# A graph attention kernel: the Sign taken from rows to columns, and the units of work cut the other way

## The reference

```
h  = max(layernorm(x), 0)
Wh = h @ W;  s = Wh @ a1;  t = Wh @ a2          # a1, a2: the halves of a
e  = leaky_relu(s[:, None] + t[None, :], 0.2)
att = softmax(where(adj > 0, e, -9e15), axis=1)
out = x + elu(att @ Wh)
```

## Time and profile before

| | |
|---|---|
| runs, median (lowest to highest) | 693.45 us (692.99 to 693.48) |
| the profiled execution, its own time | 694.66 us |
| its span, first to last instruction | 692.8 us |
| PE, DVE, ACT busy | 91%, 90%, 91% of the span |
| adj, 128 tiles of 2 MB, moved at | 427 GB/s in the loop |
| granted clock of PE, mean | 0.986 of full |

### The profile page before, as it was taken

How to read it: one execution, slowest core, us unless ns; L and a number is a source line. 1 busy time by engine, 2 the same in 40 slices (tenths; PEclk the granted TensorE clock), 3 DMA queues, 4 the chain that set the end, 5 groups by cost and what they waited for, 6 DMA issues and landing times.

```text
span 692.8 us, 23845 instructions
## 1 busy us (share of the span) xinstructions
PE 632.5 (91%) x10422; PEld 621.6 (90%) x10422; DVE 621.0 (90%) x625; ACT 631.4 (91%) x366; POOL 53.4 (8%) x51
## 2 busy tenths in 40 slices
PE   4867999999998989989898998989898998989895
PEld 4747999999998989989898998989898998989895
DVE  5898979999999899898989899898989989898983
ACT  4797999999999989989898998989899898989881
POOL 5000001011000101010010101001010100001010
PEclk9987999999999999999999999999999999999998
DMA  9876899999999999999999999999999999999960
GB/s 323 360 292 260 347 374 386 422 429 425 428 425 430 427 427 429 424 430 425 429 424 429 428 427 425 427 429 425 429 427 426 428 426 429 424 429 427 427 293 19
DMA packets 24840, 275.15 MB, mean 397 GB/s; under 512 B 3088, under 2 KB 7440, under 8 KB 8432
## 3 DMA queue, kind: packets, MB, share of 16 engines
q1 hardware_dynamic: 22864, 270.67, 93.3%
q0 software_dynamic: 1488, 4.07, 1.5%
q10 hardware_dynamic: 464, 0.07, 0.1%
HBM read 272.70 MB, written 2.10 MB: 397 GB/s over the span
## 4 chain that ended last, share of the span: by engine, by line
DMA 32%; DVE 29%; ACT 22%; issue 11%; PE 5%; DVEq 1%; ACTq 1%; SPq 0%
DMA adj_ring<-in_adj 31%; DVE code L651 18%; ACT work L513 16%; DVE work L664 4%; ACT work L521 4%; DVE code L658 1%; PE psum L876 1%; PE psum L896 1%; PE psum L894 1%; PE psum L827 1%; DMA Wx<-in_L_gnn_W 1%; PE psum L817 1%; DVE last_steps L682 1%; DVE last_steps L686 1%; ACT trow L496 1%
## 5 line engine op out<-in xcount | busy, mean ns | idle before, releaser
L896 PE MATMUL psum<-V,work 128*128 128x130 f16 x4096 | 495.3, 221 | 0.0
L894 PE MATMUL psum<-V,work 128*128 128x130 f16 x4096 | 495.0, 220 | 0.0
L513 ACT ACTIVATE work<-trow,Wh 128x4096 int8<-128x4096 f32 x128 | 476.8, 3725 | 0.0
L894 PEld LDWEIGHTS psum<-V,work 128*128 128x128 fp8e4 x4096 | 403.1, 98 | 0.0
L896 PEld LDWEIGHTS psum<-V,work 128*128 128x128 fp8e4 x4096 | 398.7, 97 | 0.0
L651 DVE TENSOR_SCALAR code<-adj_ring 128x4096 uint8<-128x4096 int32 x128 | 293.3, 2292 | 32.7 <-DMA adj_ring<-in_adj 32.7
L876 PE MATMUL psum<-identb,code 128*128 128x128 bf16 x2048 | 137.0, 220 | 41.7 <-DVE code L658 41.6
L658 DVE SCALAR_TENSOR_TENSOR code<-work,code 128x1024 int32<-128x1024 int32 x128 | 156.8, 1225 | 7.9 <-ACT work L513 4.0
L876 PEld LDWEIGHTS psum<-identb,code 128*128 128x128 bf16 x2048 | 119.8, 98 | 48.0 <-DVE code L658 30.8
L521 ACT COPY work<-psum 128x1024 int32<-128x1024 int32 x128 | 129.8, 1014 | 35.9 <-PE psum L876 35.9
L664 DVE TENSOR_SCALAR work<-work 128x1024 int32<-128x1024 int32 x128 | 87.9, 686 | 1.7 <-ACT work L521 1.7
(11 more groups left out here) (76 smaller groups left out, 151.3 us busy)
## 6 DMA issues: line engine op xcount, KB each, us to landing
adj_ring<-in_adj SPq DMA_DIRECT2D x128, 2048.0 KB, 16.9
work<-in_x SPq DMA_DIRECT2D x4, 512.0 KB, 6.0
last_steps<-in_x POOLq DMA_DIRECT2D x16, 128.0 KB, 6.6
out_y<-last_steps POOLq DMA_DIRECT2D x15, 128.0 KB, 7.8
out_y<-last_steps SPq DMA_DIRECT2D x1, 128.0 KB, 1.9
W<-in_L_gnn_W ACTq DMA_DIRECT2D x2, 16.0 KB, 5.4
Wx<-in_L_gnn_W ACTq DMA_DIRECT2D x2, 16.0 KB, 5.6
a_sb<-in_L_gnn_a ACTq DMA_DIRECT2D x1, 0.5 KB, 3.9
```

The costliest lines, as they stand in the source:

```text
L513: nc.scalar.activation(sign[:, k % 2].bitcast(I8), trow[:, h * UW:(h + 1) * UW], ACT.Sign, bias=(Wh[:, B, 0:1] if isinstance(B, int) else ...
L894: nc.tensor.matmul(sums_of[:, 0:FP], up8[:, j // 2, j % 2], V[:, jb, 0:FP], start=h == 0 and j == 0, stop=False, skip_group_check=True)
L896: last = nc.tensor.matmul(sums_of[:, FP:2 * FP], down8[:, j // 2, j % 2], V[:, jb, FP:2 * FP], start=False, stop=h == 1 and j == HB - 1, s ...
```

## The change

- A unit is now 1024 columns by all 512 rows of a body (`UW` = 1024, four blocks side by side); it still has 16 transposes and 64 products. Units 0 to 3 are the first half of the columns.
- The edge codes alone are transposed. The Sign is made in the transposed layout: partitions are columns of adj. The bias is now t of a block of 128 columns (`Wh[:, j, 2:3]`), the input a row of s of the body's 512 rows (`srow`, on all partitions). A unit takes eight Signs (`signs`) of 128 x 512, each writing every second byte. The ring of signs has four places.
- `codes` reads the sign and the transposed edge codes straight out of PSUM and writes `codeT`; `copy_unit` is gone.
- `srow` is made once a body: POOL sets four columns of s apart (`copy_scol`), PE transposes them (`srow_round`), ACT copies them out of PSUM (`copy_srow`). `trow`, `t_round` and `spread` are gone from the main path.
- `edges` runs six units ahead in the loop. In the first and the last body tiles of adj are cut by columns, and a load is two transfers.
- All eight sums of a body end in its last unit. They lie in three banks, taken by three `copy_lows` and three `take_sums`; `add_downs`, `fill_in`, `divide` and `result` follow in steps 1, 2, 3 and 5 of the next body.
- V is made in eight rounds of 8 blocks, both halves in one instruction each, one round a unit of the first body.
- Ahead of the bodies, steps of ACT, DVE and PE are put in another order.

```diff
+                def copy_srow(i):
+                    act.wait_ge(s_sp, i + 1)
+                    if not (isinstance(i, int) and i == 0):
+                        act.wait_ge(s_sign, i * BU)
+                    nc.scalar.activation(srow[:, :], first_srow_ps if isinstance(i, int) and i == 0 else srow_ps, ACT.Copy)\
+                        .then_inc(s_srow, 1)
-                def step(i, k):
-                    b, h = block_and_half(k % BU)
-                    B = (i + k // BU) * KE + b
-                    nc.scalar.activation(sign[:, k % 2].bitcast(I8), trow[:, h * UW:(h + 1) * UW], ACT.Sign,
-                                         bias=(Wh[:, B, 0:1] if isinstance(B, int) else
-                                               Wh[:, bass.ds(B, 1), 0:1].rearrange("p o f -> p (o f)")),
-                                         scale=-1.0).then_inc(s_sign, 1)
-                def copy_unit(i, k):
-                    act.wait_ge(s_mult, i * BU + k + 1)
-                    act.wait_ge(s_T, RM + i * BU + k + 1)
-                    nc.scalar.copy(codeT[:, k % RC].bitcast(I32), unitT[k % 2].bitcast(I32)).then_inc(s_codeT, 1)
+                def signs(i, k, start=0, end=UJ):
+                    static = isinstance(i, int)
+                    if start == 0 and (not static or i > 0 or k >= RS):
+                        act.wait_ge(s_code, TWO + i * BU + k - RS + 1)
+                    if start == 0 and k % BU == 0:
+                        act.wait_ge(s_srow, i + k // BU + 1)
...
+                    into = sign[:, k % RS].bitcast(I8).rearrange("p (g w b) -> p g b w", g=UG, b=2)
+                    for j in range(start, end):
+                        last = nc.scalar.activation(into[:, j // 2, j % 2], srow[:, :], ACT.Sign,
+                                                    bias=Wh[:, k % BU * UJ + j, 2:3])
+                    if end == UJ:
+                        last.then_inc(s_sign, 1)
 ACT, body:
-                        if not (last and k + 1 >= BU):
-                            copy_unit(i, k + 1)
...
-                        if not (last and k + 3 >= BU):
-                            step(i, k + 3)
+                        if first and k + 1 < NV:
+                            high_parts(k + 1)
...
+                        if k + lead == BU and not last:
+                            copy_srow(i + 1)
+                        if k == BU - 1 and not last:
+                            if first:
+                                signs(i, k + 2)
+                            signs(i, k + 3, 0, UJ // 2)
                             copy_lows(i, 0)
+                            signs(i, k + 3, UJ // 2, 3 * UJ // 4)
+                            copy_lows(i, 1)
+                            signs(i, k + 3, 3 * UJ // 4, UJ)
+                            copy_lows(i, 2)
+                        elif not (last and k + lead >= BU):
+                            signs(i, k + lead)
 DVE:
+                def codes(i, k):
+                    dve.wait_ge(s_mult, TWO + i * BU + k - 1)
+                    dve.wait_ge(s_sign, i * BU + k + 1)
                     dve.wait_ge(s_T, i * BU + k + 1)
+                    nc.vector.scalar_tensor_tensor(out=codeT[:, k % 2].bitcast(I32), in0=sign[:, k % RS].bitcast(I32),
+                                                   scalar=DOWN, in1=unitT[k % 2].bitcast(I32), op0=ALU.bitwise_xor,
+                                                   op1=ALU.bitwise_and).then_inc(s_code, 1)
+                AHEAD = {"first": [(2,), (3,), (4,), (5, 6), (7,), (8, 9), (10, 11), (12, 13)],
+                         "middle": [(k + 6,) for k in range(BU)],
+                         "last but one": [(6,), (7,), (), (), (), (8,), (9,), (10,)],
+                         "last": [(3,), (4,), (5,), (6,), (7,), (), (), ()]}
+                        if k == 0 and not first:
+                            take_sums(i - 1, 1)
+                            take_sums(i - 1, 2)
+                        if first and k + 1 < NV:
+                            products(k + 1)
                         if not (last and k + 1 >= BU):
                             codes(i, k + 1)
+                            find_ups(i, k + 1)
...
+                        if k == BU - 1:
+                            take_sums(i, 0)
+                        for n in AHEAD[which][k]:
+                            edges(i, n)
+                        if first and k + 1 < NV:
+                            low_parts(k + 1)
 PE, multiply_unit:
+                    for b in range(KE):
...
+                        bank = {0: 0, 1: 1, 3: 2}.get(b)
+                        if k == 0 and bank is not None:
+                            pe.wait_ge(s_acc[bank], ONE + i)
...
+                        if k == BU - 1 and b in (1, 2):
+                            last.then_inc(s_bank, 1)
 ACT, ahead of the bodies:
+                copy_srow(0)
+                signs(0, 0)
                 act.wait_ge(s_lim, 1)
                 t_all = Wh[:, :, 1]
                 nc.scalar.activation(uu[:, 0], t_all, ACT.Exp, bias=lim[:, 0:1]).then_inc(s_u, 1)
                 nc.scalar.activation(uu[:, 1], t_all, ACT.Exp, bias=lim[:, 1:2], scale=ALPHA).then_inc(s_u, 1)
+                signs(0, 1, 0, UJ // 2)
                 high_parts(0)
+                signs(0, 1, UJ // 2, UJ)
```

More of the change, by code:

```diff
@@ L584, in _ @@
[L584 to L590 removed]
+                signs(0, 1, UJ // 2, UJ)
                 def body(i, first=False, last=False):
+                    lead = 2 if first else 3
@@ L607, in body @@
+                        if k == 4 and not first:
                             negative_part(i - 1)
@@ L612, in _ @@
                 body(NI - 1, last=True)
-                copy_lows(NI - 1, 1)
+                for c in range(3):
+                    copy_lows(NI - 1, c)
                 negative_part(NI - 1)
@@ L676, in take_sums, with add_downs @@
+                def add_downs(i):
+                    for c in range(3):
+                        dve.wait_ge(s_acc[c], ONE + i + 1)
+                    for b in range(KE):
+                        B = i * KE + b
+                        nc.vector.scalar_tensor_tensor(out=sums[:, b], in0=parts[:, 2 * b + 1],
                                                        scalar=ab[:, B:B + 1] if isinstance(B, int) else ab[:, bass.ds(B, 1)],
-                                                       in1=parts[:, o, k, 0], op0=ALU.mult, op1=ALU.add).then_inc(s_sum2, 1)
@@ L766, in body @@
                         if not (last and k + 1 >= BU):
                             codes(i, k + 1)
-                        find_ups(i, k)
-                        if k == 1 and not first:
-                            take_sums(i - 1, 1)
-                            divide(i - 1)
-                        if k == 4 and not first:
-                            result(i - 1)
-                        if k == 7:
-                            take_sums(i, 0)
-                        if k + lead < (BU if last else BU + 2):
-                            edges(i, k + lead)
@@ L789, in body @@
                             dve.wait_ge(s_ab, 1)
-                body(0, first=True)
-                with dve.Fori(1, NI - 1) as i:
+                body(0, "first")
+                with dve.Fori(1, NI - 2) as i:
                     body(i)
-                body(NI - 1, last=True)
+                body(NI - 2, "last but one")
+                body(NI - 1, "last")
                 take_sums(NI - 1, 1)
+                take_sums(NI - 1, 2)
+                add_downs(NI - 1)
+                fill_in(NI - 1)
                 divide(NI - 1)
@@ L901, in body @@
                     for k in range(BU):
+                        if k == (4 if first else 3) and not last:
+                            if first:
+                                pe.wait_ge(s_tot, 1)
+                            pe.wait_ge(s_srow, i + 1)
+                            srow_round(i + 1, srow_ps)
                         if not (last and k + 1 >= BU):
@@ L904, in body @@
                         multiply_unit(i, k, first)
-                pe.wait_ge(s_trow, 3)
+                        if first and k < 3:
+                            for g in range(3 * k, min(3 * k + 3, JB // TR)):
+                                if g == 0:
+                                    pe.wait_ge(s_lim, 1)
+                                total(g)
                 transpose_unit(0, 0)
-                for r in range(6, JB // TR):
-                    t_round(r)
-                pe.wait_ge(s_trow, JB // TR)
                 body(0, first=True)
-                with pe.Fori(1, NI - 1) as i:
+                with pe.Fori(1, NI - 2) as i:
                     body(i)
+                body(NI - 2)
                 body(NI - 1, last=True)
```

428 lines of the change are left out of this document (220 added, 208 removed).

## The result

The changed kernel takes **731.25 us** (median of four runs, 730.72 to 733.32), the kernel before beside it 693.47 us: a ratio of 1.055, 95% interval 1.052 to 1.057. That is slower, as forecast, and 8 us above the 723 us of the prediction. The profiled execution took 733.32 us with a span of 731.5.

What follows compares the result with a forecast made beforehand. ACT was to become the bound, at 41.4 us a body: head 99.0 + loop 603.9 = 702.9, + 12.1 + 7.3 = 722.3 us of span, + 1.9 − 1.2 = 723 us. Range 700 to 752.

Steps and rivals of the forecast that it cites:

- The price of the short Sign: On ACT, a Sign over 512 elements was put at 0.615 us from start to start.
- row of 64 elements: Profile row of an Exp with a bias, followed after 0.31 us; it would put the Sign of 512 at 0.677: 781 us.
- The body on ACT: In the loop, Signs 39.4 us plus sums copies, row of s and negative part: 41.4 us a body.
- ACT is the bound: In the loop, ACT's 41.4 us a body exceeds the transfers' 39.9; chance 0.68 with Signs at 0.60 to 0.65.
- rival (a): In the loop, ACT under the bound with Signs below 0.583 us; at 0.54 about 680 us in all; chance 0.10.
- the head: From the start to the first body's end on ACT: 99.0 us with 11 units signed, no gain.
- 4 us before the first Sign: Start of the head: ACT's first Sign estimated at 24 us, between 23 and 27.
- 6 us in the first body: In the first body DVE leads with 6.4 us a step, against ACT's 4.9 + 1.0.
- The tail: After the last Sign: PE ends 12.1 us behind ACT, then 7.3 us for the sums' chain and store.
- DVE, PE, SP, POOL: In the loop, DVE under 37 us and PE 37.9 a body, hidden beneath ACT; nothing on SP's or POOL's path.
- DMA share: In the loop, the DMA engines' busy share was to be 0.96, at 410 GB/s.
- Rival (d): In first body and last unit, PE at half clock: 4 to 8 us more, 727 to 731; inside the 0.68 chance.

Runs made afterwards that it cites:

- run 7: The changed kernel with Signs written to consecutive bytes instead of every second one; one execution, 733.5 us.
- run 1: The changed kernel with seven of the eight Signs of each unit, from the fifth unit on; 705.5 us, ratio 1.017.
- run 8: The changed kernel with the eighth Sign of each unit made by GpSimd as a comparison, seven staying on ACT; 705.5 us, ratio 1.016.
- run 10: As run 9, with GpSimd also making seven of the eight products rounds of V in the first body; 701.1 us, ratio 1.012.
- run 2: The changed kernel with DVE's sums of squares of rounds 2 and 3 back behind the scalings of Wh; 729.1 us, ratio 1.051.
- run 3: The changed kernel with DVE's low parts and products of later rounds ahead of the edges in the first body; 734.0 us, ratio 1.058.
- run 4: The changed kernel with the total of Wh ahead of the edges and low parts in step 3 of the first body; 730.1 us, ratio 1.052.
- run 5: The changed kernel with DVE turning the second tile of adj right behind the first; 728.4 us, ratio 1.049.
- run 6: The changed kernel with the three copies of sums ahead of the unit's Signs in a body's last step; 729.0 us, ratio 1.052.
- run 9: The changed kernel with edits of run 2, run 4, run 5, run 6, GpSimd's comparison in six units of eight, sums before edges, no late pause; 701.5 us.
- run 11: As run 10, with all tiles of adj cut by columns and edges two units ahead; 816.1 us, ratio 1.178.
- run 12: As run 11, with edges three units ahead and two tiles in the first step; 714.7 us, ratio 1.031.

## Why the prediction was right, and where its size was off

- **The price of the short Sign: right.** 0.613 us from start to start, predicted 0.615 from the line between the Sqrt over 16 elements and the Sign over 4096. The row of 64 elements, which would have given 0.677, misled. Its source is strided, which may be why, but no run tests that. The step of two bytes costs nothing, as assumed; run 7 shows it.
- **The body on ACT: right.** 41.3 us, predicted 41.4; ACT waits nowhere in the loop. From 109.3 us to the last Sign's end at 712.2 it is 602.9 us, predicted 603.9.
- **That ACT is the bound: shown** by runs 1 and 8, each 26 us faster with one Sign in eight gone from ACT. The rest of rival (a), a lead that makes the kernel faster than before once ACT is off the path, fell: run 10 has ACT at 37.8 a body and is still 1.2% slower.
- **The term that was mis-sized: the head,** "99.0 us with 11 units signed". It measured 109.3. The other terms nearly hold (602.9, 11.8 and 7.5 against 603.9, 12.1 and 7.3), so the head is more than the whole miss: 731.5 us of span against 722.3, in an execution 2 us above the median. It has two parts.
    - *4 us before the first Sign* (28.46 against 24.5; the prediction allowed 23 to 27). The prediction counted what left ACT's order and not that DVE's reordered steps make PE wait 2.66 us for the first scaling. The edit of run 2 gives 0.6 to 3.8 us of it back, by the pattern of the head.
    - *6 us in the first body.* DVE was costed as a sum of its own instructions, 6.4 us a step, but it also waits for PE's transposes, 5.8 us in all (0.81 + 2.24 + 0.84 + 1.86). PE was put at 4.68 us a unit and hidden. Here its units also hold the total of Wh, 2.66 us, which makes 7.3 us from one unit's transposes to the next's (51.23 to 58.53), more than DVE's 6.4. And its clock was down. From the rows above, the slower transposes (twice 0.8) and products (1.4) are 3.0 us, an estimate of what the clock has in the 5.8; PE's longer unit has some 1.7 (7.3 − 6.4, twice), and the wait for the total the rest. No run separates the three. Runs 3 to 5 show that it is a ring: more waits of DVE for PE in run 3 and a later end of the body, fewer in runs 4 and 5 and an earlier one.
- **The tail: right.** PE ends 11.8 us behind ACT (12.1 predicted), and 7.5 us from there to the end (7.3). Run 6 shows part of the cause.
- **DVE, PE, SP, POOL: hidden in the loop, as predicted.** The join out of PSUM is 1.217 us long, where it was 1.225; but the ups behind it start 1.25 us after it and not 1.14. The forecast that the DMA share would fall to 0.96 was wrong: the share stays at 1.00 at 400 to 428 GB/s, though DVE never waits for a tile. DVE's waits for tiles are gone, but its long waits are for PE and for the sums rather than for Signs.
- **Rival (d), PE's clock, came true in part.** In the head it did: 0.66 from 30 to 50 us, about 3 us by the estimate above. At the boundaries it was dismissed on a row that did not cover them: the clock falls at 7 of 14, by up to half over 5 us, and it costs nothing only because ACT is slower still. That the 727 to 731 of this rival end where the time came out is luck: the clock has about 3 of the 10 us by which the head was missed.

## What to carry to other kernels

When one long instruction is cut into n short ones, cost the fixed part first: here 8 × 0.2 us of fixed part beside 8 × 0.43 us of elements made a unit that saves a whole copy dearer. Price a head that several engines share as a ring, with each engine's own sum and its waits for the others, and not as the sum of the busiest. Before two traces are compared, see that they are alike ahead of the edit: the same order of instructions gave a first row of s at 26.2 and at 28.1 us. And a lead that hides a wait in the loop is paid at the end, when the last consumer must still work it off: 33 us behind the last edges with a lead of six, 21 with three, 19 with two.

## What the runs showed of the hardware

- GpSimd takes 3.3 to 3.6 us on average for a comparison over 128 x 512 f32 with a scalar from memory and a byte output, beside a busy DVE (runs 8 to 12); single ones range from 2.0 us to 6.1 (run 10). Its product of two sources over 1040 elements took 2.0 us, as long as the shortest comparison over 512.
- A copy of four columns by GpSimd took 2.17 us at 30.3 us, beside DVE's edges, and 0.20 us at 311.4 us, where DVE was idle.
- Two waits of PE of 0.55 and 1.37 us, 2.5 us apart from start to start, were followed by a granted clock of 0.66 over the next 5 us; one body later waits of 0.58 and 1.37 us were followed by 1.00. Over the loop it was 7 boundaries of 14 each way.
- In the same order of instructions, the head of different executions put the first row of s at 26.2 to 26.4 us (three traces) or at 27.6 to 28.1 (five), by which of PE's products with Wx were slow.
- Transfers of 1 MB in runs of 4 KB moved at 407 to 409 GB/s (run 12), 2 MB in runs of 16 KB at 427 (run 10). The share of busy DMA engines shows no limit: it was 0.99 at 346 GB/s in run 11, where another ring was the bound, and 1.00 at 400 in the changed kernel, where no tile was waited for.
